# Attention and mixture-of-experts kernel on one core: TensorE's window loop written out, the first division moved into the next pair, unit 3's scores issued in unit 2 and units 0 and 1 weighed by whole products

## The reference, cut to what matters

```python
ln = layernorm(LN(x), ln_l_g, ln_l_b); xn = layernorm(ctx, ln_x_g, ln_x_b)
q = ln @ Wq                                  # 16 heads of 64
k, v = split(concat([xn, ln]) @ Wkv)         # 77 + 1024 keys per batch
sim = rmsnorm(q) * scale @ rmsnorm(k).T      # masked
x = x + (softmax(sim) @ v) @ Wout + bout
```

## Time and profile before

| what | value |
|---|---|
| profiled execution | 2599.23 us, span 2597.4 us from first to last instruction |
| median of the three runs | 2600.8 us |
| busy TensorE / weight load / VectorE / ScalarE / GpSimd | 93% / 78% / 70% / 66% / 46% of the span |
| attention pairs 0 to 31 | about 93 to 1775 us |
| mean granted TensorE clock | 0.982 |
| instruction DMA (q8) | 164 packets, 2.69 MB |

### The profile page before, as it was taken

One profiled execution on the slowest core, in us unless ns is written; L12 is line 12 of the kernel. 1 busy time (PEld: TensorE's weight loads), 2 busy tenths in 40 slices (PEclk: granted clock), 3 DMA queues, 4 the chain that ended last, 5 costly groups with the idle time before them and its releaser, 6 DMA issues. The chain is left out here.

```text
span 2597.4 us, 55511 instructions
## 1 busy us (share of the span) xinstructions
PE 2426.4 (93%) x20310; PEld 2014.8 (78%) x20310; DVE 1811.9 (70%) x2452; ACT 1705.9 (66%) x2286; POOL 1190.5 (46%) x783
## 2 busy tenths in 40 slices
PE   4799999999999999999999999997989999999998
PEld 3677677777776777777777777665989999999997
DVE  7667767677667766776667766775876566767775
ACT  2677777888887887777778777783333334444453
POOL 4334433444334433443344433442533526666665
PEclk8899999999999999999999999998999999999999
DMA  6322332233223332233223322246732459999996
GB/s 196 138 81 81 117 107 79 87 115 107 87 79 113 100 96 86 83 118 104 79 87 115 107 87 79 86 119 129 165 92 72 139 176 321 322 319 318 325 321 173
DMA packets 231564, 363.77 MB, mean 140 GB/s; under 512 B 59559, under 2 KB 139739, under 8 KB 227400
## 3 DMA queue, kind: packets, MB, share of 16 engines
q1 hardware_dynamic: 204694, 301.66, 37.7%
q0 software_dynamic: 25696, 58.82, 8.0%
q10 hardware_dynamic: 978, 0.34, 0.1%
HBM read 280.90 MB, written 79.85 MB: 139 GB/s over the span
## 5 line engine op out<-in xcount | busy, mean ns | idle before, releaser
L718 DVE TENSOR_TENSOR pr_lo<-ps_s,pr_hi 128x1024 fp32r<-128x1024 f32 x416 | 505.0, 1220 | 287.0 <-ACT ps_s L829 287.0
L828 ACT ACTIVATE pr_hi<-ps_s 128x1024 fp32r<-128x1024 f32 x512 | 526.2, 1028 | 231.9 <-PE ps_s L972 160.8
L1008 PE MATMUL ps_o<-pr_hi,vA 64*65 64x512 f32 x2292 | 489.7, 399 | 52.5 <-DVE pr_lo L718 31.6
L1008 PE MATMUL ps_o<-pr_lo,vA 64*65 64x512 f32 x2292 | 483.0, 392 | 0.0
L1008 PE MATMUL ps_o<-pr_hi,vC 64*65 64x512 f32 x2292 | 482.1, 391 | 0.0
L460 POOL TENSOR_TENSOR rs<-ss,minus_half 128x16 f32<-128x16 f32 (+1 forms) x96 | 225.7, 2351 | 480.8 <-DVE ss L693 480.8
L1666 ACT ACTIVATE ht<-f_ps_h,b 128x256 f32<-128x256 f32 x440 | 184.6, 471 | 341.6 <-PE f_ps_h L1598 341.6
L829 ACT ACTIVATE ps_s<-ps_s 128x1024 f32<-128x1024 f32 x384 | 392.5, 1022 | 0.0
L458 POOL TENSOR_TENSOR sq<-raw 128x1024 f32<-128x1024 f32 (+1 forms) x96 | 166.2, 1731 | 436.9 <-ACT raw L773 436.9
L1598 PE MATMUL f_ps_h<-xT_hi,w 128*128 128x256 f32 x1760 | 355.4, 285 | 3.6 <-DVE xT_lo L1700 3.1
L718 DVE TENSOR_TENSOR pr_lo<-pr,pr_hi 128x1024 fp32r<-128x1024 f32 x160 | 241.0, 1508 | 159.1 <-ACT pr L829 154.5
(11 more groups left out here) (220 smaller groups left out, 4611.8 us busy)
## 6 DMA issues: line engine op xcount, KB each, us to landing
w<-w1S_dram SPq DMA_DIRECT2D x160, 512.0 KB, 6.0
lnT_sb<-lnT_dram SPq DMA_DIRECT2D x31, 2304.0 KB, 9.6
w2raw<-in_L_ffn_Wproj SPq DMA_DIRECT2D x78, 512.0 KB, 6.8
w1S_dram<-cut POOLq DMA_DIRECT2D x36, 512.0 KB, 3.0
rec<-rden_dram SPq DMA_DIRECT2D x63, 256.0 KB, 3.8
routed_dram<-empty POOLq DMA_DIRECT2D x28, 387.0 KB, 3.6
xt<-routed_dram SPq DMA_DIRECT2D x39, 258.0 KB, 6.6
w_raw<-in_L_xattn_Wkv SPq DMA_DIRECT2D x66, 128.0 KB, 4.0
```

The source lines that it names most:

```text
L718: v.tensor_tensor(pr_lo[:, ring(w, d), :], full_of(d), pr_hi[:, ring(w, d), :].bitcast(F32), ALU.subtract).then_inc(s_lo, 1)
L828: act.activation(pr_hi[:, ring(w, d), :], ps_s[:, d % 2, :], ACT.Exp, bias=bias)
L1008: ins = mm(ps_o[0:DH + 1, h, :], v_[rows, h], p_[rows, 512 * h:512 * h + 512], start=k == 0 and part == 0 and i == 0, stop=k == KT - 1 and ...
```

## The change

TensorE's windows -2 to 31 of the plain body are all written out; the general body and the other engines keep the loop. The scores of unit 3 are issued in unit 2, after the second part of unit 17 of the pair before and ahead of turns 0 and 1. Behind the turns units 0 and 1 are weighed by whole products; unit 3 then issues nothing, unit 4 only its scores, turns 2 and 3 and the first part of unit 2. The division of half 0 moves from unit 16 to unit 7 of the next pair (except in the last pair), and SyncE's `store` of half 0 moves to between the next pair's `spread` and `broadcast` of half 1.

```diff
-BETWEEN = (2, 11)
+BETWEEN = 11
+WHOLE = 2
@@ SyncE, window @@
                 if w.attend and not w.first:
                     spread(w, 1, 1)
+                    store(w, 0, 1)
                     broadcast(w, 1, 1)
...
                     broadcast(w, 0, 0)
-                    store(w, 0, 0)
+                    if closing(w) and w.s == 1:
+                        store(w, 0, 0)
@@ VectorE, window @@
-                            if d == 9:
-                                divide(w, 1, 1)
+                            if d in (7, 9):
+                                divide(w, (d - 7) // 2, 1)
...
-                        if w.attend and d == 16:
+                        if closing(w) and w.s == 1 and d == 16:
                             divide(w, 0, 0)
@@ TensorE, window; the scores and their waits are now fresh(d) @@
+                    for d in range(UNITS):
+                        if d != 3:
+                            fresh(d)
...
-                        elif d in BETWEEN:
+                        elif d == 2:
+                            second(d)
+                            fresh(3)
+                            jobs(d)
+                            if w.attend:
+                                pe.wait_ge(s_v, w.n(2, 2))
+                                for e in range(WHOLE):
+                                    values(w, e)
+                        elif d == BETWEEN:
                             second(d)
                             jobs(d)
                             first(d)
-                        else:
+                        elif d != 3:
                             jobs(d)
-                            second(d)
+                            if d != 4:
+                                second(d)
                             first(d)
...
-                windows(pe, window)
+                if general:
+                    windows(pe, window)
+                else:
+                    for v in range(-1, WINDOWS // 2):
+                        for s in range(2):
+                            window(Window(v, s))
```

More of the change, by code:

```diff
@@ L1003, in values_half @@
                 else:
-                    pe.wait_ge(s_half, w.n(UNITS, d + 1))
+                    pe.wait_ge(s_half, w.n(UNITS - WHOLE, d + 1 if d < 0 else d + 1 - WHOLE))
                 for i, (v_, p_) in enumerate(pairs):
@@ L1029, in first @@
                         if w.attend and not (w.first and d < LAG):
-                            if d == LAG:
-                                pe.wait_ge(s_v, w.n(2, 2))
                             if last and d == UNITS - 1:
@@ L1035, in first, with fresh @@
                                 values_half(w, d - LAG, 0, d % 2)
-                    for d in range(UNITS):
+                    def fresh(d):
                         if w.attend:
```

## The result

The changed kernel takes 2613.99 us (median of 5, 2611.24 to 2617.69) against 2601.87 (median of 5): ratio 1.0046, 95% interval 1.0032 to 1.0061. It is slower by 0.46%, a small difference but one clear of the interval, where 2573 was forecast and the range ended at 2602. The profiled execution has a span of 2609.4 us.

What follows compares the result with a forecast made beforehand. TensorE was taken to bound the attention part. Gains 18.0 + 16.2 + 6.0 + 16.8 less costs 4.0 and 26.4 gave 26.6 us, from the profiled 2599.2 to 2572.6, so a median of 2573 us; range 2549 to 2602.

Steps and rivals of the forecast that it cites:

- Division into unit 7 with its store in the queue: SyncE's store delays rec, so VectorE stalls and unit 12's scores start late: cost 0.85 us a pair, 26.4 us.
- What bounds the kernel: Attention part: pairs run at TensorE's pace; only its 83 us of idleness, or time lost to a lowered clock, can return.
- Division out of unit 16: VectorE at lo(17), taking turns with GpSimd: TensorE's wait falls from 1.66 to 0.6 us at 17 starts, gain 18.0 us.
- TensorE written out: At the 13 jumps back: gaps go, gain 16.2 us, plus 6.0 us from the clock staying up.
- no 0.50 in the clock of the attention part: Sign of being right: TensorE's granted clock never at its lower level in the attention part.
- zero for the earlier load of lnT: SyncE's 2.3 MB load goes out some 9 us earlier, is not on the path, and costs zero.
- Scores early, whole products: TensorE in unit 2: copy of ps_o hidden, gain 16.8 us, less 4.0 us (0.13 a pair) lost in units 4 to 7.
- rival C: SyncE's write starts only once the store has landed; unit 12 starts 2.8 us late, 2633 us in all; chance 0.13.
- B: Rival: the stall for rec in unit 9 costs next to nothing, leaving gains nearly alone, 2548 to 2558 us; chance 0.20.

Runs made afterwards that it cites:

- c1: Changed kernel with write of the inverse and load of rec ahead of the store, and VectorE's sums of squares in unit 12 instead of 14: 2508.5 us, ratio 0.9650.
- c3: Kernel before with TensorE written out, new order of units 2 to 4, sums of squares in unit 12, division left in unit 16: 2504.7 us, ratio 0.9626.
- b2: Kernel before with only the moved division and its store, TensorE in its loop and old order: 2708.1 us, ratio 1.0395.
- a4: Changed kernel with TensorE back in its loop: 2682.6 us, ratio 1.0314.
- b4: Kernel before with the moved division and its store, and the load of lnT held until lo(17): 2662.5 us, ratio 1.0223.
- a2: Changed kernel with the store behind the write of the inverse and load of rec, the write still after the division: 2554.1 us, ratio 0.9819.
- a1: Changed kernel with the write of the inverse before the wait for the division, then load of rec, store last: 2550.8 us, ratio 0.9808.
- e8: Changed kernel with the division of half 0 in unit 8 instead of 7: 2741.9 us, ratio 1.0542.
- b3: Kernel before with only TensorE's new order of units 2 to 4, including whole products for units 0 and 1: 2598.5 us, ratio 0.9989.
- b1: Kernel before with only TensorE written out: 2589.0 us, ratio 0.9955.

## Why the prediction was wrong

The step that failed is the price of the moved division with its store in the queue. It was put at 26.4 us and measured 58.9. In the two profiles the kernel grew by 12.0 us where a gain of 26.6 was summed, 38.6 apart, and this term alone is 32.5 of them. Part by part:

*What bounds the kernel*: right. The losses and gains above showed as distances between TensorE's units, and none was hidden by ScalarE.

*Division out of unit 16*: right, by its mechanism. lo(17) took the division's place behind GpSimd and kept 0.53 us of wait (0.6 said). c1 shows by removal that GpSimd holds it. That the two take turns rather than share is read from the lengths shown at c1, and from the wait: 0.53 us is near the 0.6 of turns, where sharing would have left 0.3. What the step missed is what c3 shows: had GpSimd's products moved, the division could have stayed.

*TensorE written out*: right. The first ledger line is 43.7 us against 40.2, and no issue gap is left. The sign "no 0.50 in the clock of the attention part" held behind the starts of pairs but not elsewhere, see the two pairs below. The zero for the earlier load of lnT held only because TensorE is written out in the same change; with a jump left in, the load costs 2.7 us of gap at each and a lowered clock (b2, a4, b4). The prediction looked at whether the load's data were wanted, not at what else its transfer delays.

*Scores early, whole products*: right in direction, 13.0 - 6.5 = 6.5 us instead of 12.8, the second miss of the sum (6.3 us). Units 5 to 7 lost 0.21 us, not 0.13.

*Division into unit 7 with its store in the queue*: the step that failed, by its size. The mechanism, the place and the engine were as told; the price was put at 0.85 us a pair, 26.4 in all, and is 58.9. Two parts of it:

- The write of the inverse. The sum ran from 1.56 to 2.4 us between L313 and L315 and took the middle. It is 2.63, over the upper end, in nearly every pair (a2 shows that the store in front makes the difference). The rest of the chain came out near what was said: 0.88 us from the store's issue to the write's where 1.07 stood, and 3.75 us in the median from the issue of rec's load to VectorE's division where 3.8 stood. Without the two pairs below the cost is 1.50 us a pair, 43.5 in 29 pairs.
- Two pairs far outside. Pair 26 loses 6.3 us and pair 30 loses 9.1, 15 in all, which the sum didn't have. Behind both long waits the granted clock fell to the lower level, 0.51 for 6.8 us in pair 26 and 0.50 for 10.2 us in pair 30, and in pair 26 the late division met GpSimd's squares and took 2.00 us, as rival C had warned. In pair 30 the write took 7 us:

```profile
1705.38 0.69 SPq L314 DMA_DIRECT2D rden_dram<-den  x1
1712.41 0.50 SPq L316 DMA_DIRECT2D rec<-rden_dram  x1
```
```profile
1704.64 0.54 POOL L473 DMA_DIRECT2D raw<-in_L_ffn_Wfc_s  x1
...
1712.11 0.63 POOL L482 CAST cut<-raw 128x512 fp32r<-128x512 f32 x1 [6.93 <-DMA raw<-in_L_ffn_Wfc_s]
```

GpSimd's 512 KB load of expert weights was issued 0.7 us ahead of it and landed with it. That this load is the reason is argued from the rows; no run took it away. In a1, where the same load met the load of rec instead of the write, that one was late (5.26 us of wait), which speaks for it. For pair 26, where the write took 4.36 us, I have no such row, and it stays open.

Of the rivals, C was the nearest, with 0.13: it put the point of decision at 1.7 us a pair, and 1.9 was reached. Its mechanism, the write starting only when the store has landed, would have cost 2.8 and is not what happened: the load of rec goes out 3.5 us after the store's issue, where C had 5. The store lands after 3.2 us in the median, so the write ends with it. That 1.7 was passed owes something to the two pairs far outside. Had they cost 1.50 us like the others, 12 us would fall away, an estimate from the ledger: the time would stand near 2602, at the end of the range, with the term mis-sized all the same. B came out only with the queue put right: a1 measures 2551 where B said 2548 to 2558.

## What to carry to other kernels

When a step moves in a queue with a strict order, time the whole chain that now begins with it, with each small transfer priced behind the large one in front, and ask whether the large one can go last; here putting the store behind the write and the load of rec turned +12 us into -47 (a2). When one operation takes over twice its usual time, look at what runs beside it on another engine before moving its neighbour: letting GpSimd's work run two units earlier gave 51 us alone. And an edit's price depends on its company: the same loop cost 12 us or 69, and the same order of units gave 2 (with its interval, 0 to 5) or 11.

## What the runs showed of the hardware

- TensorE's jump back costs 2.0 us with idle transfer engines (DMA share 0.00 in the gaps of the kernel before and of b4) and 4.7 us with a 2.3 MB load in flight (share 0.83 in a gap of b2, 0.71 in one of a4). Its written-out form fetched 6 to 7 packets of instructions in 105 us and showed no gap of its own.
- A 4 KB write issued 0.88 us behind a 256 KB store took 2.63 us to be seen, alone 1.57.
- A subtraction of two SBUF tiles on VectorE takes 1.2 us alone and 2.7 us where GpSimd's products lie beside it; GpSimd's squares take 2.88 us there instead of 1.90 (c1).
- Behind idle stretches of TensorE of 3.9 us the granted clock was 0.50 nearly each time (e8); behind gaps of 1.8 to 2.3 us in four of 13 cases (before) and seven of 13 (b3); behind waits of 1.66 us in none of 17 (before) and none of 30 (b1), and behind waits of 1.3 to 1.5 us four times in b4. So stalls at one place can cost more than their length (e8: 128 us for 67 us of added wait, with some 17 us of longer divisions in it).
